# A decoder's merged attention stage: the output bias as a product of a row of ones on TensorE, in place of additions to the residual stream by GpSimd

## The chip, the cores and the metric

The kernel runs on one core of a Trainium2 chip. The metric is the device time of one execution in microseconds (us), the lower the better. The engines are TensorE (PE, with its weight loads shown apart as PEld), VectorE (DVE), ScalarE (ACT), GpSimd (POOL) and SyncE (SP), which issues most of the DMAs.

## The reference, cut to what matters

The program is a decoder of two layers on x of 8 batches x 512 tokens x 256 features. Each layer has an attention, a cross attention and a mixture of experts, each added to the residual stream x. The change lies in the second layer's cross attention, which has 16 heads of 16 features:

```python
    x = x + _L1_attn_ref(_layernorm(x, axis=-1), L1_attn_A, L1_attn_BC)
    x = x + _L1_xattn_ref(ctx_1024, ctx_1024, _layernorm(x, axis=-1), mask, Wv, Wk, Wq, Wo, bo)
...
    # in _L1_xattn_ref: v, k, q are heads of the three inputs, multiplied by Wv, Wk, Wq
        energy = jnp.einsum('nqhd,nkhd->nhqk', q, k)
        energy = jnp.where(mask == 0, jnp.float32(-1e+20), energy)
        attention = jax.nn.softmax(energy / jnp.sqrt(jnp.float32(E)), axis=3)
        out = jnp.einsum('nhql,nlhd->nqhd', attention, v).reshape(N, q_len, H * D)
        out = out @ Wo.T + bo
```

The vector `bo` of 256 numbers is the bias. Between the layers of the program the residual x stays in SBUF in float32, as 32 tiles of 128 tokens x 256 features, four to a batch.

## The kernel before, in words

Five stages follow one another: a first attention, a second one by correlation (stage two below, `mix_correlation`), routed experts, `mix_heads` (the stage of the change, about 945 to 1685 us of the profiled span) and the last experts.

`mix_heads` merges three things. It gathers the outputs of the routed experts into x (indirect DMAs issued by GpSimd), it runs the second layer's recurrence and adds it to x, and it runs the cross attention. Every engine has its own program, written out by hand, and they meet through semaphores that only count up.

The work goes batch by batch (8), in each batch by four groups g of four heads, in each group by eight steps n. At a step TensorE does two units of second energies (keys by queries, line 1105, into the PSUM tile `slim` of three slots, which ACT turns into exponentials, line 1278) and, between them, a pair of first energies for work half a group ahead (line 1094, into the PSUM tile `wide` of two slots, from which DVE takes row maxima, line 1349). After steps 1, 3, 5 and 7 it multiplies exponentials and values (line 1117; four products side by side, each on 32 of the array's columns). The table constants of lines 741 to 751 place everything else between these steps: `PREP_AT` prepares the next batch, `REC_AT` is the recurrence of the batch after the next, and `FIN_AT` = ((1, 1), (1, 4), (2, 1)) finishes the batch before. So in each batch b, `finish(b - 1)` on TensorE (lines 1135 to 1150) turns the heads' outputs in group 1, step 1; does output products for two tiles in group 1, step 4; and for the other two in group 2, step 1. I call the last two **output steps**: there are two a batch, 16 in all. In each of them TensorE does, for two tiles j, two products of 128x128 by 128x256 in float32 (line 1148) that add up in PSUM. A float32 product is two TensorE instructions in the trace, so an output step is 8 of them. DVE then adds the 128x512 result to x (line 1374) and takes statistics of it (line 1378). The last batch's three finishing items stand behind all other work (lines 1228 to 1231).

`wide` has two slots that are used in turn by energies, preparation, finishing and recurrence. TensorE waits before each use for the engine that empties the slot (`wide_freed`, line 807).

The bias is loaded by SP (line 920) as 128 copies of the 256 numbers. GpSimd adds it to the four tiles of a batch in x (`add_bias`, lines 995 to 1000). For batch 0 that stands between its part of the preparation and the gathers (line 1034); for batch b + 1 it stands at the end of group 3 of batch b (line 1053), behind `max_rows`. The latter is the end of a chain: DVE's maxima, split by GpSimd in three bfloat16 parts (lines 1008 to 1014), turned by TensorE (line 1125), copied by DVE (line 1355), and sent by a DMA on GpSimd's queue (line 1020) into the rows that the next group's second energies read. DVE waits for the addition in its `finish` (line 1372).

At the same place, in group 3, steps 5 to 7 of batches 0 to 5, DVE computes means and variances for the next normalization (`mean_of` and `var_of`, lines 1408 to 1422: short instructions in a chain, each waiting for the one before), ACT takes the root (line 1298) between two loads of its function table, and DVE goes on with a reciprocal and the normalizations (lines 1428, 1324).

Stage two already adds its own output bias as a product, for each of 8 batches: `nc.tensor.matmul(o, ones[0:1, :], bo[:], start=False, stop=True)` (line 553) behind two products of 128 rows (line 552), all in float32 with 256 columns.

Of the kernel before, what the change touches and what calls it, by code (L numbers as in the profile page):

```python
# [16 lines left out]
P = 128  # L17
B, S, D = 8, 512, 256
NT = B * S // P
TB = S // P  # L20
DC = D // P
# [638 lines left out]
def mix_heads(nc, ctx, x, ident, ident_bf, stats, mean, rstd, ctx_in, mask_in, w_vT, w_kT, w_qT, w_oT, b_o, part_rows, mask_dram,  # L660
# [6 lines left out]
    with ExitStack() as own:  # L667
        k = Kit(nc, own, "hd_")
        s = Kit(nc, ctx, "hd_")
        H, DH = 16, 16  # L670
        GH = 4
        NG = H // GH
# [12 lines left out]
        wq = k.sb("wq", [P, P])  # L685
        wv = k.sb("wv", [P, P])
        wo = k.sb("wo", [P, DC, D])
        bias = k.sb("bias", [P, D])
        parts = k.sb("parts", [P, 2, 3, DC, S], BF16)
        rest = k.sb("rest", [P, 2, DC, S])  # L690
        k_stack = k.sb("k_stack", [ROWS, 2, H, S], BF16)
# [1 line left out]
        zero = k.sb("zero", [P, 1])  # L693
# [9 lines left out]
        nparts = k.sb("nparts", [P, 2, P // (GH * TB), GH * TB], BF16)  # L703
        nrows = k.sb("nrows", [3 * GH * TB, 2, P], BF16)
        prob = k.sb("prob", [P, NUNIT, S])
        ones_bf = prob[0:ROWS - MASK_ROW, 0, :].bitcast(BF16)[:, 0:S]
# [6 lines left out]
        wide = k.ps("wide", [P, 2, 2, S])  # L713
        slim = k.ps("slim", [P, 3, S])
        pv = k.ps("pv", [P, S])
        zeroed, loaded, blocks_ready, weights_ready = s.sem("zeroed"), s.sem("loaded"), s.sem("blocks_ready"), s.sem("weights_ready")
        ones_ready, ones_loaded = s.sem("ones_ready"), s.sem("ones_loaded")
        ctx_loaded = s.sem("ctx_loaded")
        xn_ready, bias_added = s.sem("xn_ready"), s.sem("bias_added")
        wide_full, turned_ready, v_ready, maxed = s.sem("wide_full"), s.sem("turned_ready"), s.sem("v_ready"), s.sem("maxed")  # L720
        part0_ready, rest_ready, part1_ready, part2_ready = s.sem("part0_ready"), s.sem("rest_ready"), s.sem("part1_ready"), s.sem("part2_ready")
        stored, stacked, masked = s.sem("stored"), [s.sem(f"stacked{g}") for g in range(NG)], s.sem("masked")
# [8 lines left out]
        mask_loaded, rec_loaded, out_loaded = s.sem("mask_loaded"), s.sem("rec_loaded"), s.sem("out_loaded")  # L731
# [148 lines left out]
        with nc.Block() as block:  # L880
            @block.sync
            def _(sp):
# [34 lines left out]
                sp.dma_start(mask, mask_in.rearrange("b x y s -> (b x y) s")).then_inc(mask_loaded, 16)  # L917
                sp.dma_start(wbc[:], w_bc.rearrange("(c p) n -> p c n", p=P)).then_inc(rec_loaded, 16)
                sp.dma_start(decay[:], decay_in.rearrange("(c p) -> p c", p=P), allow_slow_non_contiguous=True).then_inc(rec_loaded, 16)
                sp.dma_start(bias[:], b_o.rearrange("(a n) -> a n", a=1).to_broadcast([P, D])).then_inc(out_loaded, 16)  # L920
                sp.dma_start(wo[:], w_oT.rearrange("(c p) n -> p c n", p=P)).then_inc(out_loaded, 16)

                sp.wait_ge(zeroed, 1)
# [39 lines left out]
            def _(pool):  # L963
# [28 lines left out]
                    pool.wait_ge(part1_ready, b * 2 + a + 1)  # L992
                    nc.gpsimd.tensor_tensor(parts[:, a, 2], rest[:, a], parts[:, a, 1], ALU.subtract).then_inc(part2_ready, 1)

                def add_bias(b):

                    pool.wait_ge(xn_ready, b * TB + TB)
                    for j in range(TB):
                        last = nc.gpsimd.tensor_tensor(x[:, b * TB + j, :], x[:, b * TB + j, :], bias[:], ALU.add)
                    last.then_inc(bias_added, 1)  # L1000

                def split_max(bt, g):

                    m, p = nmax[:, g % 2], nparts[:, g % 2].rearrange("p n (h c) -> p n h c", h=GH)
                    at = (bt.b * NG + g) * 3
                    z = zero[:].unsqueeze(2).to_broadcast([P, GH, TB])
                    pool.wait_ge(maxed, (bt.b * NG + g) * NSTEP + NSTEP)
                    nc.gpsimd.tensor_tensor(p[:, 0], m, z, ALU.add).then_inc(nstep, 1)
                    pool.wait_ge(nstep, at + 1)
                    nc.gpsimd.tensor_tensor(nrest[:], m, p[:, 0], ALU.subtract).then_inc(nstep, 1)  # L1010
                    pool.wait_ge(nstep, at + 2)
                    nc.gpsimd.tensor_tensor(p[:, 1], nrest[:], z, ALU.add).then_inc(nstep, 1)
                    pool.wait_ge(nstep, at + 3)
                    nc.gpsimd.tensor_tensor(p[:, 2], nrest[:], p[:, 1], ALU.subtract).then_inc(nparts_ready, 1)
# [8 lines left out]

                ALL = TB * TOP
                gathered_rows(0, range(TB))
                pool.wait_ge(zeroed, 3)
                pool.wait_ge(ones_loaded, 32)
                pool.wait_ge(mask_stored, 16)
                pool.sem_inc(passed, 1)
                gathered_rows(1, range(TB))  # L1030
                third_part(0, 0)
                pool.wait_ge(out_loaded, 32)
                third_part(0, 1)
                add_bias(0)
                gathers(2, 0, ALL // 2)
                split_max(Batch(0, 0), 0)
                max_rows(Batch(0, 0), 0)
                for b in range(B):
                    bt, nxt = Batch(b, b % 2), Batch(b + 1, (b + 1) % 2)
                    for g in range(NG):  # L1040
                        if g < NG - 1:
                            split_max(bt, g + 1)
                            max_rows(bt, g + 1)
                        elif b < B - 1:
                            split_max(nxt, 0)
                            max_rows(nxt, 0)
                        if g == 0 and b == 0:
                            gathers(2, ALL // 2, ALL)
                        if g == 0 and b < B - 1:
                            third_part(b + 1, 0)  # L1050
                            third_part(b + 1, 1)
                        if g == NG - 1 and b < B - 1:
                            add_bias(b + 1)
                        if bt.gathers and g < NG - 1:
                            gathers(b + 3, (0, 6, 13)[g], (6, 13, ALL)[g])
                for sem in nrows_loaded:
# [3 lines left out]
            def _(pe):  # L1060
# [74 lines left out]
                def finish(b, slot, n, at):  # L1135

                    if n == 0:
                        pe.wait_ge(turned, b * NG + NG)
                        for c in range(DC):
                            for qc in range(TB):  # L1140
                                last = nc.tensor.transpose(wide[:, at, c, qc * P:(qc + 1) * P], o[:, slot, qc, c * P:(c + 1) * P], ident[:])
                    else:
                        pe.wait_ge(out_loaded, 32)
                        pe.wait_ge(out_turned, b + 1)
                        for j in range(2):
                            qc = 2 * (n - 1) + j
                            for c in range(DC):
                                last = nc.tensor.matmul(wide[:, at, 0, j * D:(j + 1) * D], oT2[:, c, qc * P:(qc + 1) * P], wo[:, c, :],
                                                        start=(c == 0), stop=(c == DC - 1))
                    last.then_inc(wide_full, 1)  # L1150

                def combine(r, item, at):
# [167 lines left out]
            def _(dve):  # L1320
# [3 lines left out]
                        nc.vector.tensor_scalar(xn[:, j, :], x[:, t, :], mean[:, bass.ds(t, 1)], rstd[:, bass.ds(t, 1)],  # L1324
                                                ALU.subtract, ALU.mult).then_inc(xn_ready, 1)

                for t, value in ((ones_bf, 1.0), (nparts[:], 0.0), (zero[:], 0.0)):
                    nc.vector.memset(t, value).then_inc(zeroed, 1)
                dve.wait_ge(loaded, 3 * 16)
                dve.wait_ge(blocks_ready, 3)  # L1330
# [37 lines left out]

                def finish(b, n, uses, at):
                    dve.wait_ge(wide_full, uses + 1)  # L1370
                    if n == 1:
                        dve.wait_ge(bias_added, b + 1)
                    xs = x[:, bass.ds(b * TB + 2 * (n - 1), 2), :].rearrange("p j n -> p (j n)")
                    nc.vector.tensor_tensor(xs, xs, wide[:, at, 0, :], ALU.add).then_inc(x_done, 1)
                    dve.wait_ge(x_done, b * 2 + n)
                    for j in range(2):
                        t = b * TB + 2 * (n - 1) + j
                        nc.vector.bn_stats(stats[:, t, :], x[:, t, :]).then_inc(stats_done, 1)
# [1332 lines left out]
```

## Time and profile before

| | |
|---|---|
| median of 3 runs | 2698.16 us (2696.84 to 2705.11) |
| the profiled execution's own time | 2706.32 us |
| its span in the profile | 2704.3 us |
| PE busy | 2299.8 us (85%), 12186 instructions |
| PEld busy | 1627.9 us (60%) |
| DVE busy | 1270.6 us (47%) |
| ACT busy | 848.1 us (31%) |
| POOL busy | 866.2 us (32%) |

Times of the trace count from the start of the span. A slice of the page is 67.6 us. In the windows view, the numbers behind a stretch are its length and then the busy time and number of instructions of PE, PEld, DVE, ACT and POOL, the clock granted to TensorE as a share of 2.4 GHz, the share of the DMA engines and GB/s. In a timeline, a line gives start and length in us, engine, source line, operation, output and inputs, how many instructions were merged, and in brackets the idle time of the engine before it with what ended it. Matmul instructions overlap, so their pace is read from starts.

### The profile page before, as it was taken

The numbers are of one execution on the slowest core, as the hardware profiler recorded it, in microseconds if no ns is written. First come the engines' busy times: TensorE is split into PE (matmuls) and PEld (weight loads), VectorE is DVE, ScalarE is ACT, GpSimd is POOL, SyncE is SP. The second block draws the span as 40 slices with busy tenths as digits, with TensorE's granted clock in tenths as the row PEclk, the third lists the DMA queues.
The fourth block names the chain that finished last, engine by engine and source line by source line (L and its number), as shares of the span: only waits on it lengthen the run. The fifth ranks groups of instructions, "written<-read, shape, count | busy, mean of one in ns | idle before, by whom it ended". The sixth has DMA issues, their size and how long they took to land. (4 is left out here: it accounts for less than half of the span.)

```text
span 2704.3 us, 39994 instructions
## 1 busy us (share of the span) xinstructions
PE 2299.8 (85%) x12186; PEld 1627.9 (60%) x12187; DVE 1270.6 (47%) x2717; ACT 848.1 (31%) x1915; POOL 866.2 (32%) x1109
## 2 busy tenths in 40 slices
PE   6998856673999926698888887999999999999998
PEld 3454834442777722243333333655589999999998
DVE  5554135344444446677677765379322222222222
ACT  2222202220444403455565565322212222222221
POOL 2000003563000043654344121122235444445544
PEclk9999656886999967899899999999999999999999
DMA  9993116222555543544334220410047777777775
GB/s 338 372 365 133 58 28 249 86 95 81 157 156 156 152 125 83 106 111 101 71 73 102 67 72 13 162 39 16 16 139 245 246 245 245 246 249 247 247 246 168
DMA packets 246074, 412.60 MB, mean 153 GB/s; under 512 B 29958, under 2 KB 223855, under 8 KB 237784
## 3 DMA queue, kind: packets, MB, share of 16 engines
q1 hardware_dynamic: 206040, 351.70, 38.4%
q0 software_dynamic: 39936, 59.70, 10.7%
q8 instruction: 49, 0.80, 0.1%
q14 instruction: 49, 0.40, 0.0%
HBM read 261.83 MB, written 148.89 MB: 152 GB/s over the span
## 5 line engine op out<-in xcount | busy, mean ns | idle before, releaser
L2544 PE MATMUL me_hp<-me_xgT,me_w 128*128 128x160 f32 x3072 | 440.2, 300 | 0.6 <-DVE me_xgT L2586 0.6
L2544 PEld LDWEIGHTS me_hp<-me_xgT,me_w 128*128 128x128 f32 x3072 | 424.6, 191 | 1.5 <-DVE me_xgT L2586 0.7
L1349 DVE TENSOR_REDUCE hd_nmax<-hd_wide 128x2 f32<-128x1024 f32 x256 | 307.7, 1219 | 128.5 <-PE hd_wide L1094 124.3
L1278 ACT ACTIVATE hd_prob<-hd_slim 128x512 f32<-128x512 f32 x512 | 276.2, 601 | 190.4 <-PE hd_slim L1105 157.6
L2600 DVE TENSOR_TENSOR me_hid<-me_act_out,me_hp 128x160 f32<-128x160 f32 x384 | 123.5, 322 | 371.8 <-ACT me_act_out L2572 354.2
L1105 PE MATMUL hd_slim<-hd_q_stack,hd_k_stack 100*128 100x512 bf16 x512 | 199.9, 394 | 43.1 <-ACT hd_prob L1278 32.8
L2553 PE MATMUL me_op<-me_hid,me_w 128*128 128x160 f32 x1536 | 235.9, 303 | 0.0
L1094 PE MATMUL hd_wide<-hd_k_stack,hd_q_stack 97*128 97x512 bf16 x512 | 201.3, 398 | 29.5 <-DVE hd_rest L1343 15.9
L2572 ACT ACTIVATE me_act_out<-me_hp 128x160 f32<-128x160 f32 x384 | 116.8, 304 | 346.0 <-PE me_hp L2544 346.0
L2553 PEld LDWEIGHTS me_op<-me_hid,me_w 128*128 128x128 f32 x1536 | 213.7, 190 | 2.6
L1105 PEld LDWEIGHTS hd_slim<-hd_q_stack,hd_k_stack 100*128 100x128 bf16 x512 | 50.2, 99 | 197.7 <-ACT hd_prob L1278 84.7
L1977 PE MATMUL mr_e_hp<-mr_w,mr_e_xtT 128*128 x640 | 167.9, 385 | 0.8 <-issue 0.8
L2244 PE MATMUL me_r_hp<-me_r_xnT,me_r_sw 128*128 128x512 f32 x384 | 167.5, 592 | 0.0
L977 POOL DMA_INDIRECT all_x<-outputs,rt_place x96 | 150.2, 1565 | 28.4 <-issue 28.4
L1665 POOL DMA_INDIRECT places<-mr_s_xg,mr_s_place x128 | 124.9, 976 | 89.5 <-DVE mr_s_place L1825 50.4
L1117 PE MATMUL hd_pv<-hd_prob,hd_v 128*32 128x512 f32 x1024 | 137.7, 610 | 3.9 <-ACT hd_oT L1241 3.6
L2202 POOL TENSOR_TENSOR me_r_hid<-me_r_act_out,me_r_up_out 128x512 f32<-128x512 f32 x48 | 64.5, 1345 | 211.6 <-ACT me_r_up_out L2300 211.6
L2490 POOL DMA_INDIRECT out_x<-me_oa,me_then_a x64 | 104.1, 1626 | 69.5 <-POOL me_then_b L2096 35.7
L2244 PEld LDWEIGHTS me_r_hp<-me_r_xnT,me_r_sw 128*128 128x128 f32 x384 | 72.3, 190 | 84.6 <-issue 84.2
L2033 DVE TENSOR_TENSOR mr_e_hid<-mr_e_act_out,mr_e_hp 128x128 f32<-128x128 f32 x160 | 46.1, 288 | 153.7 <-ACT mr_e_act_out L2009 153.7
L1977 PEld LDWEIGHTS mr_e_hp<-mr_w,mr_e_xtT 128*128 128x128 f32 x640 | 110.4, 193 | 10.5 <-issue 1.5
L2574 ACT ACTIVATE me_oT<-me_op 128x320 f32<-128x320 f32 x64 | 28.0, 437 | 242.1 <-PE me_op L2553 242.1
(384 smaller groups left out, 3731.2 us busy)
## 6 DMA issues: line engine op xcount, KB each, us to landing
me_w<-in_L_ffn_w_exp SPq DMA_DIRECT2D x64, 2304.0 KB
places<-z_zero SPq DMA_DIRECT2D x64, 1152.0 KB, 11.2
mr_e_xt<-places SPq DMA_DIRECT2D x160, 144.0 KB, 2.2
outputs<-mr_e_y SPq DMA_DIRECT2D x160, 128.0 KB, 1.7
part_rows<-hd_parts SPq DMA_DIRECT2D x48, 256.0 KB
hd_k_stack<-part_rows SPq DMA_DIRECT2D x192, 64.0 KB
hd_q_stack<-part_rows SPq DMA_DIRECT2D x192, 64.0 KB
mr_w<-in_L_ffn_w_in SPq DMA_DIRECT2D x4, 2048.0 KB
```

Of the source, the lines that this page charges most:

```text
L977: nc.gpsimd.indirect_dma_start(out=x[:, r * TB + j, :], out_offset=None, in_=outputs[:, :], in_offset=bass.IndirectOffsetOnAxis(ap=place[: ...
L1094: last = nc.tensor.matmul(wide[:, at, j, :], q_stack[0:FIRST_ROWS, bt.slot, h, qc * P:(qc + 1) * P], k_stack[0:FIRST_ROWS, bt.slot, h, :], ...
L1105: nc.tensor.matmul(slim[:, slim_slot(bt, item), :], k_stack[:, bt.slot, h, kc * P:(kc + 1) * P], q_stack[:, bt.slot, h, :], start=True, st ...
L1117: last = nc.tensor.matmul(pv[32 * j:32 * j + 32, :], v[:, slot, kc, head(g, j), :], prob[:, kc * GH + j, :], start=(kc == 0), stop=(kc == ...
L1278: nc.scalar.activation(prob[:, u, :], slim[:, slim_slot(bt, item), :], ACT.Exp, scale=D ** -0.5)\
L1349: nc.vector.tensor_reduce(nmax[:, g % 2, n // 2, c:c + 2], wide[:, at], AX.X, ALU.max, negate=True)\
L1665: nc.gpsimd.indirect_dma_start(out=places[:, :], out_offset=bass.IndirectOffsetOnAxis(ap=place[:, b * TB + j, n:n + 1], axis=0), in_=xg[:, ...
L1977: last = nc.tensor.matmul(hp[:, v, 0:2 * F], xtT[:, v, c, :], w1[:, bass.ds(e, 1), c, :].rearrange("p a n -> p (a n)"), start=(c == 0), st ...
L2244: last = nc.tensor.matmul(hp[:, u % 2, half, :], sw1[:, c, at:at + P], xnT[:, c, b * S:(b + 1) * S], start=(c == 0), stop=(c == DC - 1))
L2544: last = nc.tensor.matmul(hp[:, f % 3, half * CAP:(half + 1) * CAP], w1[:, sl, c, cols], xgT[:, sl, c, :], start=(c == 0), stop=(c == DC - 1))
L2553: last = nc.tensor.matmul(op[:, c, 0:CAP], w2[:, sl, f, c * P:(c + 1) * P], hid[:, sl, f, :], start=(f == 0), stop=(f == FC - 1))
L2600: nc.vector.tensor_tensor(hid[:, sl, f, :], act_out[:, f % 2, :], hp[:, f % 3, 0:CAP], ALU.mult).then_inc(h_free, 1)
```

## The change

The bias and a new row of 128 ones have one partition each. DVE sets the ones (a fourth small memset), SP loads the bias once. GpSimd's additions, their semaphore and DVE's wait for it go. In each output step TensorE begins each of its two sums with a product of the row of ones (1x128) and the bias (1x256), in float32, as in stage two.

```diff
-        bias = k.sb("bias", [P, D])
+        bias = k.sb("bias", [1, D])
+        one_row = k.sb("one_row", [1, P])
...
-        xn_ready, bias_added = s.sem("xn_ready"), s.sem("bias_added")
+        xn_ready = s.sem("xn_ready")
...
-                sp.dma_start(bias[:], b_o.rearrange("(a n) -> a n", a=1).to_broadcast([P, D])).then_inc(out_loaded, 16)
+                sp.dma_start(bias[:], b_o.rearrange("(a n) -> a n", a=1)).then_inc(out_loaded, 16)
...
-                def add_bias(b):
-
-                    pool.wait_ge(xn_ready, b * TB + TB)
-                    for j in range(TB):
-                        last = nc.gpsimd.tensor_tensor(x[:, b * TB + j, :], x[:, b * TB + j, :], bias[:], ALU.add)
-                    last.then_inc(bias_added, 1)
-
...
-                pool.wait_ge(zeroed, 3)
+                pool.wait_ge(zeroed, 4)
...
                 third_part(0, 0)
-                pool.wait_ge(out_loaded, 32)
                 third_part(0, 1)
-                add_bias(0)
                 gathers(2, 0, ALL // 2)
...
-                        if g == NG - 1 and b < B - 1:
-                            add_bias(b + 1)
...
+                        pe.wait_ge(zeroed, 4)
                         pe.wait_ge(out_loaded, 32)
                         pe.wait_ge(out_turned, b + 1)
                         for j in range(2):
+                            nc.tensor.matmul(wide[:, at, 0, j * D:(j + 1) * D], one_row[:], bias[:], start=True, stop=False)
                             qc = 2 * (n - 1) + j
                             for c in range(DC):
                                 last = nc.tensor.matmul(wide[:, at, 0, j * D:(j + 1) * D], oT2[:, c, qc * P:(qc + 1) * P], wo[:, c, :],
-                                                        start=(c == 0), stop=(c == DC - 1))
+                                                        start=False, stop=(c == DC - 1))
...
-                for t, value in ((ones_bf, 1.0), (nparts[:], 0.0), (zero[:], 0.0)):
+                for t, value in ((ones_bf, 1.0), (nparts[:], 0.0), (zero[:], 0.0), (one_row[:], 1.0)):
...
                     dve.wait_ge(wide_full, uses + 1)
-                    if n == 1:
-                        dve.wait_ge(bias_added, b + 1)
```

## Rows read from the trace of the kernel before

**Rows 1.** The page in 40 slices: PE busy and granted clock, in tenths.

```profile
PE   6998856673999926698888887999999999999998
...
PEclk9999656886999967899899999999999999999999
```

**Rows 2.** Windows: us, busy us (x) per engine, granted clock, DMA share, GB/s.

```profile
1180.00:1260.00 80.00, 68.67 (x364) 30.38 (x361) 57.45 (x82) 46.53 (x81) 38.30 (x47) 0.96 0.41 92
```

**Rows 3.** Line and tile views: duration ns (min/median/max), first and last start.

```profile
L1148 PE MATMUL hd_wide<-hd_wo,hd_oT x128: 377/379/483, 1182.1 to 1683.4; 128*128 128x256 f32 x128
...
L999 POOL TENSOR_TENSOR all_x<-all_x,hd_bias x32: 716/738/769, 1025.8 to 1619.7; 128x256 f32<-128x256 f32 x32
```

**Rows 4.** Timeline at a first output step: start, us, engine, line, operation, [idle before].

```profile
1262.65 1.89 PE L1148 MATMUL hd_wide<-hd_wo,hd_oT 128*128 128x256 f32 x8
...
1264.38 0.60 PE L1132 MATMUL hd_slim<-all_ident,hd_oT 128*128 128x128 f32 x4
...
1266.38 0.65 PE L1157 MATMUL hd_wide<-all_ident,hd_xn 128*128 128x128 f32 x4 [0.53 <-DVE all_x L1374]
```

**Rows 5.** Timeline at the second output step of the same batch.

```profile
1276.05 1.99 PE L1148 MATMUL hd_wide<-hd_wo,hd_oT 128*128 128x256 f32 x8 [0.44 <-DVE hd_nmax L1349]
...
1277.97 1.06 PE L1117 MATMUL hd_pv<-hd_prob,hd_v 128*32 128x512 f32 x8
```

**Rows 6.** Timeline and window of stage two, where a bias is already a product.

```profile
393.59 1.22 PE L553 MATMUL xa_proj<-xa_bo,xa_ones 1*128 1x256 f32 x2
...
396.74 1.22 PE L553 MATMUL xa_proj<-xa_bo,xa_ones 1*128 1x256 f32 x2
...
398.00:402.00 4.00, 4.00 (x8) 2.40 (x9) 3.67 (x11) 0.00 (x0) 0.00 (x0) 0.50 0.00 0
```

**Rows 7.** Timeline of DVE at the start of the attention stage.

```profile
959.09 0.29 DVE L1332 TENSOR_TENSOR hd_wk<-hd_wk,hd_blocks 128x128 f32<-128x128 f32 x1 [5.26 <-DMA hd_wv<-in_L_xattn_WvT]
```

**Rows 8.** DVE groups, 1100 to 1660 us: busy, mean ns; then L1414 alone.

```profile
L1413 DVE TENSOR_SCALAR all_mean<-all_mean (+2 forms) x6 | 3.6, 605 | 0.2
...
L1414 DVE TENSOR_TENSOR hd_half_diff<-all_stats 128x8 f32 (+2 forms) x6 | 3.9, 650 | 0.2
...
L1415 DVE SCALAR_TENSOR_TENSOR hd_half_diff<-hd_half_diff 128x8 f32<-128x8 f32 (+1 forms) x6 | 3.8, 636 | 0.2
...
L1421 DVE SCALAR_TENSOR_TENSOR hd_var<-hd_var,hd_half_diff 128x8 f32<-128x8 f32 (+1 forms) x6 | 1.4, 239 | 0.2
...
L1414 DVE TENSOR_TENSOR hd_half_diff<-all_stats x11: 165/643/656, 981.1 to 1545.2; 128x4 f32<-128x4 f32 x6, 128x8 f32 x4, 128x8 f32<-128x8 f32 x1
```

**Rows 9.** Timeline where a bias addition meets the end of a batch.

```profile
1222.74 2.77 POOL L999 TENSOR_TENSOR all_x<-all_x,hd_bias 128x256 f32<-128x256 f32 x4
...
1226.74 0.21 ACT L1298 ACTIVATE hd_dev<-hd_var 128x8 f32<-128x8 f32 x1 [2.90 <-DVE hd_var L1422]
...
1228.91 0.61 PE L1105 MATMUL hd_slim<-hd_q_stack,hd_k_stack 100*128 100x512 bf16 x1 [2.25 <-ACT hd_prob L1278]
```

**Rows 10.** Timeline at the first bias addition; below it the same DVE form undisturbed.

```profile
1024.34 3.84 DVE L1436 TENSOR_SCALAR hd_xn<-all_x,all_mean,all_rstd 128x256 f32<-128x256 f32 x4
...
1028.33 1.09 PE L1157 MATMUL hd_wide<-all_ident,hd_xn 128*128 128x128 f32 x4 [8.37 <-DVE hd_xn L1436]
...
1228.00 1.38 DVE L1324 TENSOR_SCALAR hd_xn<-all_x,all_mean,all_rstd 128x256 f32 x4
```

**Rows 11.** Window and GpSimd timeline behind two ends of a batch.

```profile
1304.00:1322.00 18.00, 12.14 (x44) 5.73 (x41) 9.13 (x15) 8.64 (x14) 1.94 (x3) 0.62 0.11 34
...
1302.43 0.70 POOL L1020 DMA_DIRECT2D hd_q_stack<-hd_nrows  x1
...
1332.54 0.65 POOL L1020 DMA_DIRECT2D hd_q_stack<-hd_nrows  x1
...
1466.59 0.71 POOL L1020 DMA_DIRECT2D hd_q_stack<-hd_nrows  x1
...
1492.13 0.66 POOL L1020 DMA_DIRECT2D hd_q_stack<-hd_nrows  x1
```

## The prediction

> **What bounds the kernel now.** I began with the page's slices. The stage of the change is slices 16 to 25: TensorE is busy for 80 to 90% of nearly every one, at close to full clock [rows 1]. A window of one steady batch says the same: PE 68.7 of 80 us, against 57.5 for DVE, 46.5 for ACT and 38.3 for POOL [rows 2]. So work added to TensorE is suspected of costing its full length, and work taken from GpSimd of being worth nothing by itself. Whether that holds is a matter of the two places where the work lies, so I read those in the timeline next.
>
> At an output step TensorE has no gap: the 8 instructions start at 1262.65 and the next work, turning a group's output, follows at 1264.38. 2.00 us later, at 1266.38, TensorE has waited 0.53 us for DVE's addition to x [rows 4]. That addition reads what TensorE wrote and stands on DVE behind the normalization of the group just turned. A later end of the output step makes turning, DVE and this wait later by the same amount; it doesn't fill the gap. At the second output step TensorE waits 0.44 us before it, for a slot that DVE empties, and the new products wait for that slot too [rows 5]. I find no event behind an output step that TensorE waits for and that doesn't itself follow from TensorE's work.
>
> At the ends of batches, GpSimd's addition is not the bystander that its idle time suggests. It starts at 1222.74, while DVE is in its chain of statistics [rows 9], and three of these instructions, of 8 columns each, take 605 to 650 ns on the mean where the undisturbed ones take 165 [rows 8]. ACT waits 2.90 us for the end of that chain, then loads its table, and TensorE waits 2.25 us for ACT's first exponential [rows 9]. So here GpSimd's work is on the path.
>
> **What the change adds.** Two products in each of 16 output steps (128 instructions of line 1148 are 16 steps of 8 [rows 3]) are 32 products, 64 instructions of 256 columns in float32. Undisturbed such an instruction takes (1264.38 - 1262.65) / 8 = 0.216 us [rows 4]: 0.86 us a step, 13.8 us in all.
>
> They have one row where their neighbours have 128 (or 97). Stage two shows what such a product costs between products of 128 rows: a batch of 4 + 2 instructions takes 396.74 - 393.59 = 3.15 us, at a granted clock of 0.50, that is 1.2 GHz [rows 6]. At that clock six instructions should take 6 x 0.432 = 2.59 us. The 0.56 us left are two changes of shape, 0.28 us each. The nearest row at full clock (2.4 GHz) is the output step that begins behind a wait, with its weights not loaded ahead, and ends at line 1117, whose products use 32 columns each: 1277.97 - 1276.05 = 1.92 us for 8 instructions, 0.19 more than 8 x 0.216 [rows 5]. A change of shape seems to have both of these, loads that aren't ahead and a gap, and the clock of the output steps is full, so I take 0.19. Bounds: nothing (no row excludes it at 2.4 GHz) and 0.28 (if it is a fixed time). An output step has four changes (into the row, out, in, out), 0.76 us, 12.2 us over 16 steps. The sum added is 13.8 + 12.2 = **26.0 us**, from 13.8 to 31.7.
>
> By the Trainium skill, "TensorEngine Tiling (Array Packing)", section "Key Properties", changing the tiling mode makes TensorE drain. Its page "TensorE: Matmul & The Clock Gate", section "Single matmul latency", puts a drain at some 175 ns; by that estimate the 64 changes would add 11.2 us. The rows of stage two agree that there is such a price; no row here shows it with one row at full clock.
>
> All of it lies on the path by the reading above, the last batch's two steps too, behind which only DVE works. The wait for the ones is passed long before; nothing is queued behind it that could run. The memset is the fourth of DVE's small ones, and DVE idles 5.26 us behind them for weights; without that cover it would cost under 0.1 us [rows 7]. GpSimd waits for it at a point far ahead of its next use. The smaller load of the bias costs nothing and gives nothing: no one but the first output step, 200 us later, needs it now. DVE's wait that goes was met each time, since the addition lies more than a batch before it.
>
> **What it removes.** GpSimd loses 32 x 0.738 = 23.6 us of work [rows 3], which is worth what it held up:
> - The statistics of batches 0 to 5. The excess over 0.165 us is 2.6 + 2.9 + 2.8 + 0.4 = 8.8 us (6 x 0.440, 0.485, 0.471, 0.074) [rows 8]. In batch 5, whose chain starts before the addition, one instruction of line 1414 is slowed by the issue of a DMA by GpSimd and stays so, 0.5 us by the mean of its line: 8.3 us. It is on the path through ACT to TensorE [rows 9]. With the chain 1.4 us shorter (0.44 + 0.485 + 0.47) the next thing late is still ACT's table and the exponential, 0.85 us of the 2.25 us wait being left, so I take it all. Bounds: 0 and 8.3 us.
> - The first addition. DVE's four normalizations take 3.84 us, undisturbed 1.38, and TensorE waits for them [rows 10]. They begin under another instruction of GpSimd, which stays; from its end at about 1025.9 the last three need 1.0 us instead of 2.3. I take 1.1 us, between 0 and 2.5.
>
> The gathers that GpSimd issues behind the first addition start 3 us earlier; those that DVE waits for in batch 0 stand behind a later DMA of maxima, and gain nothing of it. The sum removed is **9.4 us**.
>
> **The clock** may move either way. Behind the ends of batches it falls; in the worst window (18 us) it averages 0.62, with PE busy for 12.14 us [rows 11]. From one DMA of maxima to the next this boundary takes 1332.54 - 1302.43 = 30.1 us, another 25.5 [rows 11]. A stall shorter by 1.4 us might avoid the fall; a shift of the work against it might lengthen it. With 30.1 against 25.5 as the ends, six boundaries hold some 12 us to be regained at best (4.6 from the worst, an estimated 1.5 from each other), and about as much to be lost. I take 0.
>
> **Sum:** 26.0 - 9.4 = +16.6 us; against the profiled execution's 2706.3 us that is 2722.9. This execution was 8.2 us over the median of the runs shown, and I put the difference to the median: 2698.2 + 16.6 = **2714.8 us**, 0.6% slower. A measurement of this kernel can tell about 0.3%, 8.1 us, from no change.
>
> **Rivals.**
> - *The products are absorbed.* TensorE idles 11 us in a batch [rows 2]; if its stalls at the end of a batch (2.25 us for ACT and others [rows 9]) are set by DVE, ACT and DMAs rather than by its own progress, the 3.2 us a batch vanish in them. Then only the removed 9.4 us show: 2688.8 us, **faster**. It decides the sign from 64% absorbed (26.0 x 0.36 = 9.4) and passes -0.3% where all but 1.3 us is. Against it: the statistics and maxima that set those stalls wait for TensorE's energies of the same group, which shift too. 6%.
> - *A change of shape costs nothing at full clock.* Then 13.8 - 9.4 = +4.4 us: 2702.6, no change that can be told. For it: the only rows with one row are at half clock. Against it: the gap at line 1117, which is at full clock [rows 5]. 13%. By the Trainium skill, "TensorE: Matmul & The Clock Gate", section "Why this matters for your kernels", a single product of 32 rows takes as long as one of 128; that would be this case.
> - *The clock comes back.* The shorter stalls keep TensorE at 2.4 GHz: 16.6 - 12 = +5 us, 2703. It needs the falls behind most ends of a batch to go. 9%.
> - *The dear change.* 0.28 us each at any clock: 31.7 - 9.4 = +22.3 us, 2720.5. 12%.
>
> **How the numbers follow.** The forecast has 60%. Its own range, with the clock at +-6 us and the gains at their lower bounds in part, is 2707 to 2722. To leave out no more than 2 in 10 the range takes in the cheap change and the regained clock below, and the dear change with some loss of clock above: 2702 to 2725. Slower by over 0.3% (above 2706.3): the forecast but for a twelfth of it, the dear change, and part of the regained clock, 69%. Within 0.3%: 26%. Faster by over 0.3%: the absorbed case but for its last part, 5%.
>
> **What the next profile should show.** Line 1148's 128 instructions unchanged, and 64 new ones of 1x256; an output step from its first start to the next work of about 3.4 us instead of 1.73 (2.6 if the change of shape is free); POOL's busy time down by 24 us; the statistics' instructions at 165 to 185 ns; TensorE's wait for the exponential at the end of a batch about 1.5 us shorter; the batch as a whole about 1.8 us longer. The forecast is wrong if the output step grows by 1.6 us and the batch doesn't (absorbed), if it grows by 0.9 (cheap change), or if the windows behind the ends of batches have another clock.

## The result and the profile after

| | before | after |
|---|---|---|
| median, 13 runs each on one chip | 2699.9 us (2692.8 to 2707.5) | 2719.1 us (2707.0 to 2732.2) |
| ratio to before, 95% interval | | 1.0068 (1.0048 to 1.0088) |
| profiled execution, its span | 2706.3, 2704.3 us | 2722.1, 2719.8 us |

The change costs 18.4 us (13.0 to 23.8) by the ratio and 15.5 us by the two spans. The page of the changed kernel, busy times and slices:

```profile
PE 2323.3 (85%) x12250; PEld 1633.4 (60%) x12251; DVE 1260.3 (46%) x2718; ACT 847.3 (31%) x1915; POOL 842.3 (31%) x1077
...
PE   6998856674999835788888888899999999999998
...
PEclk9999566886999957999999999899999999999999
```

GpSimd is busy for 23.9 us less, TensorE for 23.5 us more. The slices of the stage look like [rows 1]: little of it is visible at this scale but the clock, whose two slices of 0.8 in the stage before now read 0.9, and which has a slice of 0.8 behind the stage's end. So I went to the same four places as before.

**The output steps**, in TensorE's timeline of the changed kernel (first and second output step of one batch), and the tile view of the new products:

```profile
1259.10 0.38 PE L1084 MATMUL hd_wide<-hd_k_stack,hd_q_stack 97*128 97x512 bf16 x1
1259.40 0.69 PE L1137 MATMUL hd_wide<-hd_bias,hd_one_row 1*128 1x256 f32 x2
1260.03 1.13 PE L1140 MATMUL hd_wide<-hd_wo,hd_oT 128*128 128x256 f32 x4
1261.09 0.69 PE L1137 MATMUL hd_wide<-hd_bias,hd_one_row 1*128 1x256 f32 x2
1261.71 1.13 PE L1140 MATMUL hd_wide<-hd_wo,hd_oT 128*128 128x256 f32 x4
1262.68 0.60 PE L1122 MATMUL hd_slim<-all_ident,hd_oT 128*128 128x128 f32 x4
...
1274.35 0.69 PE L1137 MATMUL hd_wide<-hd_bias,hd_one_row 1*128 1x256 f32 x2 [0.44 <-DVE hd_nmax L1341]
...
1277.72 1.07 PE L1107 MATMUL hd_pv<-hd_prob,hd_v 128*32 128x512 f32 x8
```

```profile
L1137 PE MATMUL hd_wide<-hd_bias,hd_one_row x64: 374/478/792, 1178.0 to 1697.1; 1*128 1x256 f32 x64
```

From the first start to the next work, the first step takes 1262.68 - 1259.40 = 3.28 us, in place of 1.73 [rows 4]; the second takes 3.37, in place of 1.92 [rows 5]. The wait of 0.44 us ahead of the second is still there, unchanged. The starts within the first step show where the time beyond the columns goes: from the two instructions of one row to the next work it is 0.63 us, 0.20 more than 2 x 0.216, and from the four of 128 rows to the next pair 1.06 us, 0.20 more than 4 x 0.216. Either shape pays when it follows the other, so this is a price of the change and not of a product of one row by itself.

**The statistics of DVE**, groups of 1100 to 1660 us of the changed kernel (busy, mean ns):

```profile
L1403 DVE TENSOR_SCALAR all_mean<-all_mean (+2 forms) x6 | 1.0, 174 | 0.2
L1404 DVE TENSOR_TENSOR hd_half_diff<-all_stats 128x8 f32 (+2 forms) x6 | 1.0, 172 | 0.2
...
L1405 DVE SCALAR_TENSOR_TENSOR hd_half_diff<-hd_half_diff 128x8 f32<-128x8 f32 (+1 forms) x6 | 1.0, 167 | 0.2
```

They took 605, 650 and 636 ns before [rows 8]. **The end of a batch**, in the timeline of the changed kernel, with the DMA of maxima at three ends of a batch; the line of before's GpSimd timeline that answers to the first of them stands below it:

```profile
1222.46 0.70 POOL L1014 DMA_DIRECT2D hd_q_stack<-hd_nrows  x1
...
1225.73 0.21 ACT L1290 ACTIVATE hd_dev<-hd_var 128x8 f32<-128x8 f32 x1 [1.45 <-DVE hd_var L1412]
...
1227.90 0.39 PE L1095 MATMUL hd_slim<-hd_q_stack,hd_k_stack 100*128 100x512 bf16 x1 [1.73 <-ACT hd_prob L1270]
...
1302.19 0.70 POOL L1014 DMA_DIRECT2D hd_q_stack<-hd_nrows  x1
...
1331.06 0.65 POOL L1014 DMA_DIRECT2D hd_q_stack<-hd_nrows  x1
...
1469.39 0.71 POOL L1014 DMA_DIRECT2D hd_q_stack<-hd_nrows  x1
...
1493.71 0.66 POOL L1014 DMA_DIRECT2D hd_q_stack<-hd_nrows  x1
```

```profile
1222.01 0.71 POOL L1020 DMA_DIRECT2D hd_q_stack<-hd_nrows  x1
```

ACT waits 1.45 us for the statistics, not 2.90 [rows 9]. From the DMA to the energies behind ACT's first exponential it is 1227.90 - 1222.46 = 5.44 us; before it was 1228.91 - 1222.01 = 6.90 [rows 9]. That is 1.46 us less for one end of a batch.

**The start and the tail of the stage**: DVE's first normalizations and TensorE behind them, then the last batch's output steps, in the changed kernel's timeline; below, before's last output steps.

```profile
1022.69 2.72 DVE L1426 TENSOR_SCALAR hd_xn<-all_x,all_mean,all_rstd 128x256 f32<-128x256 f32 x4
...
1025.56 1.94 PE L1149 MATMUL hd_wide<-all_ident,hd_xn 128*128 128x128 f32 x8 [7.11 <-DVE hd_xn L1426]
...
1688.78 0.67 PE L1137 MATMUL hd_wide<-hd_bias,hd_one_row 1*128 1x256 f32 x2 [1.21 <-ACT hd_oT L1259]
...
1697.69 2.08 PE L1140 MATMUL hd_wide<-hd_wo,hd_oT 128*128 128x256 f32 x4
```

```profile
1680.09 3.69 PE L1148 MATMUL hd_wide<-hd_wo,hd_oT 128*128 128x256 f32 x16 [1.20 <-ACT hd_oT L1267]
```

The last two output steps took 3.69 us and now take 1699.77 - 1688.78 = 11.0 us. The windows of the changed kernel (columns as in [rows 2]) show a second reason beside the products: the clock is 0.61 there, the third line.

```profile
1180.00:1260.00 80.00, 69.54 (x368) 28.99 (x366) 55.75 (x82) 46.67 (x81) 34.60 (x42) 0.98 0.40 89
1304.00:1322.00 18.00, 12.61 (x52) 6.01 (x52) 7.97 (x14) 9.42 (x16) 0.00 (x0) 0.72 0.10 34
1688.00:1700.00 12.00, 10.98 (x24) 5.79 (x24) 1.64 (x4) 0.64 (x1) 0.00 (x0) 0.61 0.00 0
```

So the trace of the change already holds both halves of the forecast: a longer output step and a shorter end of a batch. What it can't show is how much of the 18.4 us each is worth, since one execution differs from another by several us in stages that the change doesn't touch. That is what the runs below are for.

### The profile page after: what moved, and what is told of

Same layout as the page of the kernel before. It is cut to its first block and busy times, and to the rows that moved or that the text cites. A ratio compares the mean times of both kernels' runs of the same rounds, so it can differ in the third digit from the quotient of the medians.

```text
span 2719.8 us, 40098 instructions
## 1 busy us (share of the span) xinstructions
PE 2323.3 (85%) x12250; PEld 1633.4 (60%) x12251; DVE 1260.3 (46%) x2718; ACT 847.3 (31%) x1915; POOL 842.3 (31%) x1077
## 6 DMA issues: line engine op xcount, KB each, us to landing
mr_e_xt<-places SPq DMA_DIRECT2D x160, 144.0 KB, 2.1
```

## The experiments

My theory: the products cost their full length, a good part of which is the change of shape to one row and back, and the end of GpSimd's collision with DVE gives back some 10 us. The rivals: the gain is larger than the collision (the clock comes back) and the products dearer; or a bias product costs its columns alone, and the rest of the time is something else. Experiments 1 to 4 ran on one chip, where before took 2700.4 us (29 runs); 5 and 6 on another, where the same kernel took 2652.9 us (11 runs). Only ratios are carried from one to the other.

### 1. The additions taken away, no products

```diff
-                            nc.tensor.matmul(wide[:, at, 0, j * D:(j + 1) * D], one_row[:], bias[:], start=True, stop=False)
...
-                                                        start=False, stop=(c == DC - 1))
+                                                        start=(c == 0), stop=(c == DC - 1))
```

Against the changed kernel. Nothing adds the bias: this part of the computation is left out.

> The changed kernel without its products of the row of ones, so that no one adds the bias: GpSimd's additions are gone and TensorE's program is that of before. The output lacks the bias in every token. It measures the gain of the removal alone. By my sum: the statistics 8.3 us and the first addition 1.1 us, so 9.4 us faster than before, about 2690. By the traces compared (the ends of batches were 14.7 us shorter in all, the stretch before the first batch about 1.4 us), with falls of the clock that went away: 14 to 17 us faster, about 2684. By the rival for which GpSimd's idle time shows that its work is hidden: no change, 2700. The statistics' instructions take 165 to 175 ns in either of the first two.

Measured: 2688.4 us (12 runs), ratio 0.9963 (0.9945 to 0.998), that is -10.0 us (-14.9 to -5.4). The statistics are at 172 ns, in DVE's groups of this kernel:

```profile
L1403 DVE TENSOR_TENSOR hd_half_diff<-all_stats 128x8 f32 (+2 forms) x6 | 1.0, 172 | 0.2
```

So the additions, which ran on an engine that is idle for two thirds of the time, cost about 10 us. The forecast's 9.4 us holds. Of the rival's 14 to 17 us the interval leaves only the lowest part: 17 is out, 14 just isn't.

### 2. The additions kept, and products of a row of zeros besides

```diff
+        no_row = k.sb("no_row", [1, P])
...
+                            nc.tensor.matmul(wide[:, at, 0, j * D:(j + 1) * D], no_row[:], bias[0:1, :], start=True, stop=False)
...
-                                                        start=(c == 0), stop=(c == DC - 1))
+                                                        start=False, stop=(c == DC - 1))
```

Against the kernel before. The zeros are a fourth memset; the sums don't change.

> The kernel before, with all its additions, plus a product of a row of zeros and the bias ahead of each of the 32 sums: the cost of the products alone. By my sum 26.0 us slower, 2726. If TensorE's stalls absorb them: under 10 us slower. If the products also lower the clock, as the changed kernel's last output steps suggest (11.0 us instead of 3.7 where the sum has 7.0): 28 to 35 us slower. An output step of group 1 takes 3.28 us at full clock, one of group 2 3.37 us.

Measured: 2728.4 us (6 runs), ratio 1.0107 (1.0085 to 1.0129), +28.9 us (23.0 to 34.8). TensorE's timeline at a second output step, and DVE's group of the statistics, in this kernel:

```profile
1279.57 0.69 PE L1148 MATMUL hd_wide<-hd_bias,hd_no_row 1*128 1x256 f32 x2 [0.44 <-DVE hd_nmax L1352]
...
1282.94 1.06 PE L1118 MATMUL hd_pv<-hd_prob,hd_v 128*32 128x512 f32 x8
```

```profile
L1417 DVE TENSOR_TENSOR hd_half_diff<-all_stats 128x8 f32 (+2 forms) x6 | 3.9, 650 | 0.2
```

The step is the changed kernel's (3.37 us), the statistics are before's (650 ns). The two halves add up: 28.9 - 10.0 = 18.9 us, and the whole change measures 18.4. Each half is known to some 5 us, so a third effect larger than that isn't there; a smaller one isn't excluded. Between 26.0 and the rival's 28 to 35 us the interval doesn't decide.

### 3. Products of 128 rows in place of one

```diff
-        bias = k.sb("bias", [1, D])
-        one_row = k.sb("one_row", [1, P])
+        bias = k.sb("bias", [P, D])
+        one_row = k.sb("one_row", [P, P])
...
-                sp.dma_start(bias[:], b_o.rearrange("(a n) -> a n", a=1)).then_inc(out_loaded, 16)
+                sp.dma_start(bias[:], b_o.rearrange("(a n) -> a n", a=1).to_broadcast([P, D])).then_inc(out_loaded, 16)
...
-                for t, value in ((ones_bf, 1.0), (nparts[:], 0.0), (zero[:], 0.0), (one_row[:], 1.0)):
+                for t, value in ((ones_bf, 1.0), (nparts[:], 0.0), (zero[:], 0.0), (one_row[:], 1.0 / P)):
```

Against the changed kernel: 128 rows of 1/128 by 128 copies of the bias. The instructions are as many and have as many columns; only the shape is that of their neighbours.

> The changed kernel with 128 rows of 1/128 and the bias on all 128 partitions, float32 as before: the same number of instructions and columns, but no change of shape. If the change of shape is what an instruction of one row costs beyond its columns, an output step takes 1.73 + 0.86 = 2.6 us in group 1 and 2.8 us in group 2, 11 us less over 16 steps: about 7 us slower than before, 2707. If the clock also stops falling behind output steps and in the last ones, 14 to 18 us less than the changed kernel: equal to before within 4 us. If the price comes from something else (accumulating on a third product, the semaphore wait), no change against the changed kernel: 18 us slower than before.

Measured: 2705.5 us (12 runs), ratio 1.0025 (1.0009 to 1.004), +6.8 us (2.4 to 10.8); 11.6 us less than the whole change. TensorE's timeline of this kernel at a first output step:

```profile
1253.71 0.38 PE L1084 MATMUL hd_wide<-hd_k_stack,hd_q_stack 97*128 97x512 bf16 x1
1253.93 0.60 PE L1137 MATMUL hd_wide<-hd_bias,hd_one_row 128*128 128x256 f32 x2
...
1256.52 0.60 PE L1122 MATMUL hd_slim<-all_ident,hd_oT 128*128 128x128 f32 x4
```

The step takes 1256.52 - 1253.93 = 2.59 us: 12 instructions of 0.216. Against the changed kernel's 3.28, and 0.22 instead of 0.30 us from the last energies to it, the row shape costs 0.69 + 0.08 = 0.77 us in a first output step, 0.19 for each of four changes. Nothing else differs in what TensorE does, so more rows, and with them 128 times the arithmetic, are cheaper than one.

### 4. One row still, but two changes of shape in a step instead of four

```diff
-        bias = k.sb("bias", [1, D])
+        bias = k.sb("bias", [1, 2, D])
...
-                sp.dma_start(bias[:], b_o.rearrange("(a n) -> a n", a=1)).then_inc(out_loaded, 16)
+                sp.dma_start(bias[:], b_o.rearrange("(a j n) -> a j n", a=1, j=1).to_broadcast([1, 2, D])).then_inc(out_loaded, 16)
...
+                        nc.tensor.matmul(wide[:, at, 0, :], one_row[:], bias[:].rearrange("a j n -> a (j n)"), start=True, stop=False,
+                                         skip_group_check=True)
                         for j in range(2):
-                            nc.tensor.matmul(wide[:, at, 0, j * D:(j + 1) * D], one_row[:], bias[:], start=True, stop=False)
```

Against the changed kernel: one product of 512 columns for both tiles. The columns are the same.

> The changed kernel with the bias stored twice in its row and one product of 512 columns a step in place of two of 256: as many columns, half the changes of shape. By the price per change (0.17 to 0.19 us each, two fewer a step) an output step is 0.35 us shorter, 5.5 us in all: 13 us slower than before, 2713. If the price is per product and not per change, the same 5 us; if it lies in the columns (a product of one row streams slowly), nothing. The pace inside the product tells the last two apart: 0.43 us between the starts of its two instructions at full clock, if it streams as others do.

Measured: 2709.9 us (12 runs), ratio 1.0033 (1.0012 to 1.0055), +8.9 us (3.2 to 14.8). TensorE's timeline of this kernel:

```profile
1253.36 0.38 PE L1084 MATMUL hd_wide<-hd_k_stack,hd_q_stack 97*128 97x512 bf16 x1
1253.67 1.12 PE L1136 MATMUL hd_wide<-hd_bias,hd_one_row 1*128 1x512 f32 x2
1254.72 1.99 PE L1141 MATMUL hd_wide<-hd_wo,hd_oT 128*128 128x256 f32 x8
1256.55 0.60 PE L1122 MATMUL hd_slim<-all_ident,hd_oT 128*128 128x128 f32 x4
```

2.88 us: 0.40 less than the changed kernel, for two changes fewer, 0.20 each. Over 16 steps that is 6.3 us of the 9.5 by which the medians' ratios differ; the intervals take in the rest. The two instructions of one row take 1254.72 - 1253.67 = 1.05 us for 1024 columns, which is 4 x 0.216 and one change: their columns are no slower than others. Experiment 4 by itself can't tell a price for each change from one for each product, since it halves both. The starts in the changed kernel's output step do, and experiment 3 shows that as many products without a change of shape cost their columns alone.

### 5. The additions kept on GpSimd, but moved out of DVE's way

```diff
-                def add_bias(b):
+                def add_bias(b, normed):
...
-                    pool.wait_ge(xn_ready, b * TB + TB)
+                    pool.wait_ge(xn_ready, normed)
...
-                add_bias(0)
...
                 max_rows(Batch(0, 0), 0)
+                add_bias(0, 2 * TB)
...
-                            add_bias(b + 1)
+                            add_bias(b + 1, min(b + 3, B) * TB)
```

Against the kernel before. If the 10 us of experiment 1 are the collision and not GpSimd's work as such, they are to be had with all 32 additions in place: they only have to start behind DVE's normalization of the next batch.

> The kernel before with GpSimd's additions kept, each moved behind the next batch's normalization, where DVE is in none of its statistics; TensorE has no product for the bias. If the gain of the removal (10.0 us measured) was the collision with DVE's chain of statistics, it comes back in full here although GpSimd does all its work: 8 to 11 us faster than before, 2690, and the statistics' instructions take 165 to 180 ns. If it came from GpSimd having less to do at all (its queue, its DMAs), no change against before. If the additions now stand in the way of the third parts or the splits of maxima that follow on GpSimd, slower than before by up to 2.8 us a batch.

Measured: 2640.6 us (5 runs) against 2652.9, ratio 0.9962 (0.9948 to 0.9976), -10.1 us (-13.8 to -6.4). DVE's group of the statistics; GpSimd's timeline at an end of a batch, in this kernel:

```profile
L1414 DVE TENSOR_TENSOR hd_half_diff<-all_stats 128x8 f32 (+2 forms) x6 | 1.0, 172 | 0.2
```

```profile
1160.56 0.70 POOL L1020 DMA_DIRECT2D hd_q_stack<-hd_nrows  x1
1166.58 2.77 POOL L999 TENSOR_TENSOR all_x<-all_x,hd_bias 128x256 f32<-128x256 f32 x4 [5.31 <-DVE hd_xn L1324]
...
1184.68 0.65 POOL L1020 DMA_DIRECT2D hd_q_stack<-hd_nrows  x1
```

The same 2.77 us of additions, 5.3 us later, and the whole gain of experiment 1. From one DMA to the next it takes 24.1 us. By the ratios this version is faster than both kernels of the case.

### 6. The product in its cheapest shape

```diff
-        bias = k.sb("bias", [1, D])
-        one_row = k.sb("one_row", [1, P])
+        bias = k.sb("bias", [P, D])
+        bias_rows = k.sb("bias_rows", [P, 2, D], BF16)
+        one_row = k.sb("one_row", [P, P], BF16)
...
+                        nc.tensor.matmul(wide[:, at, 0, :], one_row[:], bias_rows[:].rearrange("p j n -> p (j n)"), start=True, stop=False,
+                                         skip_group_check=True)
                         for j in range(2):
-                            nc.tensor.matmul(wide[:, at, 0, j * D:(j + 1) * D], one_row[:], bias[:], start=True, stop=False)
...
+                    steps.link(nc.vector.tensor_copy(part[:, 0], bias[:]))
+                    steps.link(nc.vector.tensor_tensor(rest[:, 0], bias[:], part[:, 0], ALU.subtract))
+                    steps.link(nc.vector.tensor_copy(part[:, 1], rest[:, 0]))
+                    steps.link(nc.vector.tensor_tensor(rest[:, 1], rest[:, 0], part[:, 1], ALU.subtract))
+                    steps.link(nc.vector.tensor_scalar(rest[:, 0], part[:, 0], ident[:, 0:1], None, ALU.mult))
+                    steps.link(nc.vector.scalar_tensor_tensor(rest[:, 0], part[:, 1], ident[:, 1:2], rest[:, 0], ALU.mult, ALU.add))
+                    steps.link(nc.vector.scalar_tensor_tensor(rest[:, 0], rest[:, 1], ident[:, 2:3], rest[:, 0], ALU.mult, ALU.add))
+                    steps.link(nc.vector.tensor_copy(bias_rows[:, 0], rest[:, 0]))
+                    steps.tick(nc.vector.tensor_copy(bias_rows[:, 1], rest[:, 0]))
```

Against the changed kernel. Once, at the stage's start, DVE splits the bias into three bfloat16 parts and puts them in rows 0, 1 and 2 of a tile of 128 rows, the others zero. With ones in bfloat16 a step then has one instruction of 512 columns, without a change of shape.

> The changed kernel with the bias product in its cheapest form: the bias split once in three bfloat16 parts that stand in rows 0 to 2 of a tile of 128 rows (the rest zero), two copies side by side, against a full tile of ones in bfloat16: one instruction of 512 columns a step, no change of shape. An output step takes 0.22 us more than before, 3.5 us over 16 steps, and the removal gives 10: 6 to 7 us faster than before, 2693, and 25 us faster than the changed kernel. The nine short instructions of DVE that make the parts lie in its wait for weights and gathers at the start of the stage and cost at most 3 us. If the mere presence of a third product in the sum costs time, not its columns and its shape, an output step grows by over 0.5 us and the gain is under 2 us.

Measured: 2639.7 us (6 runs) against 2652.9, ratio 0.9959 (0.9944 to 0.9974), -10.9 us (-14.9 to -6.9). TensorE's timeline of this kernel, and the tile view of the new operand's loads (15 of the 16 instructions themselves are missing from the records):

```profile
1204.78 0.38 PE L1086 MATMUL hd_wide<-hd_k_stack,hd_q_stack 97*128 97x512 bf16 x1
1205.21 1.89 PE L1144 MATMUL hd_wide<-hd_wo,hd_oT 128*128 128x256 f32 x8
1206.94 0.60 PE L1124 MATMUL hd_slim<-all_ident,hd_oT 128*128 128x128 f32 x4
```

```profile
L1139 PEld LDWEIGHTS hd_wide<-hd_bias_rows,hd_one_row x16: 95/95/98, 1126.5 to 1615.7; 128*128 128x128 bf16 x16
```

From the last energies to the first product of line 1144 it is 0.43 us, where experiment 3's first two lines stand 0.22 apart: the instruction adds 0.21 us to a first output step. Around a second one it adds 0.13: from one DMA of maxima to the next it is 20.10 us there and 19.97 in experiment 5, which has no product. That is 2.7 us in all, not the 3.5 expected, and would leave 10.0 - 2.7 = 7.3 us of gain. The interval, 6.9 to 14.9, holds that at its lower end; most of it lies above the 6 to 7 us expected, and why isn't explained. The gain isn't distinguishable from experiment 5's, and by the ratios this version too is faster than both kernels of the case.

## Why the prediction was right, step by step

The forecast was slower, by 16.6 us, to 2714.8; measured were 2719.1 us and +18.4 (13.0 to 23.8).

- **TensorE has no room at the output steps**: right. Neither step absorbed any of the products, and the wait of 0.44 us ahead of the second kept its length. The absorbed case is out by experiment 2.
- **Products, 13.8 us**: right. Experiment 3 shows 0.216 us for each of its 12 instructions in a step.
- **Changes of shape, 0.19 us each, 12.2 us**: right in the price, one too many in every second step. In the first step the four cost 0.19 each (experiment 3). The second step grew by 3.37 - 1.92 = 1.45 us, 0.86 of it columns, and the 0.59 left are three changes. The fourth was paid before already: it is the very 0.19 from which the forecast took its price [rows 5]. Counted in the trace of the change, seven batches of 1.55 + 0.08 + 1.45 = 3.08 us and an estimated 3.2 us at full clock for the last steps make 24.8 us, beside the forecast's 26.0 and experiment 2's 28.9 (23.0 to 34.8). The cheap case, 13.8, and the dear one as a fixed 0.28 us at any clock are out, both by the steps of 3.28 and 2.88 us. The ones' memset takes 0.165 us where under 0.1 was forecast; it still lies in DVE's wait for the weights.

The Trainium skill says in "TensorEngine Tiling (Array Packing)", section "Key Properties", that changing the tiling mode drains TensorE. The trace agrees with a price at such a change, close to the 175 ns that the Trainium skill has for a drain in "TensorE: Matmul & The Clock Gate", section "Single matmul latency"; that the 0.19 us are this drain is not shown. By the Trainium skill, the same page, section "Why this matters for your kernels", a single product of 32 rows takes as long as one of 128. Here, with one row, that holds for the columns (experiment 4) but not for a product between others of 128 rows.

- **The statistics, 8.3 us, and the first addition, 1.1 us**: right, with one misreading. Experiment 1 shows 10.0 us for both, the end of a batch shows 1.46 us less where 1.4 were forecast, and the first four normalizations take 2.72 instead of 3.84 us [rows 10], 1.12 less. Experiment 5 shows that the gain is the collision's: it comes in full with all additions in place. The misreading: I took 0.5 us of batch 5 for the work of a DMA issue and kept it. In the changed kernel the same instruction lies wholly under the same issue and takes 0.17 us. Its two timelines there, DVE's and GpSimd's:

```profile
1549.89 0.17 DVE L1404 TENSOR_TENSOR hd_half_diff<-all_stats 128x4 f32<-128x4 f32 x1
```

```profile
1549.78 0.62 POOL L1014 DMA_DIRECT2D hd_q_stack<-hd_nrows  x1
```

So that 0.5 us went as well, and the sum of the collision should have been 8.8.

- **The clock, 0 by choice between -12 and +12**: the term without a reading of its own, and that 0 served was luck. In the two profiled executions the clock moved both ways. The six ends of a batch (DMA of maxima to the next) take 158.9 us before and 144.0 after, 14.9 less, of which the chain explains 8.8. In the profiles of the experiments they take 158.6 us with the collision (2), and without it 146.3 (1), 146.4 (3), 147.8 (4), 146.2 (5) and 143.3 (6). So wherever the collision is gone some 2 to 7 us beyond the chain come back (5 and 6 ran on the other chip). In the change the worst went from 30.1 [rows 11] to 28.9 us, with its window's clock from 0.62 to 0.72.

  Against that, the clock fell in output steps. In the changed kernel two of the seven stretches around a second output step take 23.0 us from DMA to DMA where the others like them take 21.4 (from 1185.60 to 1208.60, for one, with a clock of 0.74 from 1196 to 1202), which is 3.2 us. The last output steps grew by 7.3 us, an estimated 3.2 for the products and 4.1 for the clock of 0.61. With the counted terms, 24.8 + 3.2 + 4.1 - 14.9 - 1.1 = 16.1 us, the 15.5 us between the two spans are nearly all named. Experiment 1, which has no bias product, fell in the last steps too; its window and timeline:

```profile
1650.00:1655.00 5.00, 4.33 (x12) 3.53 (x13) 1.02 (x2) 0.52 (x1) 0.00 (x0) 0.66 0.00 0
```

```profile
1650.67 5.38 PE L1139 MATMUL hd_wide<-hd_wo,hd_oT 128*128 128x256 f32 x16 [1.21 <-ACT hd_oT L1258]
```

  So a fall in the last steps isn't the products' doing alone. But the three kernels with products of one row (the change, 2 and 4) have the lowest mean clocks over these steps, 0.59, 0.60 and 0.63, where experiment 1 has 0.68, 3 has 0.76 and before, 5 and 6 have 1.00. They are also the only ones with a fall around a second output step of the seven batches before: two, one and one, and none in the five other profiles. One profile of each isn't proof, so that such products bring falls with them is not shown; it would explain why experiment 2 measured 28.9 us where the steps count 24.8. How large the clock's shifts are in most of the 13 runs, and what makes a fall come in one execution and not in another, stays open.

- **A batch 1.8 us longer**: the two batches from 1302 to 1469 us take 1469.39 - 1302.19 = 167.2 us, before 164.2 [rows 11], 1.5 us each. In that sum are falls of the clock that went and one that came, so it isn't the chain and the steps alone. That the 80 us window shows TensorE busy for only 0.9 us more than [rows 2] is no sign against it: the window holds another piece of the batch.
- **TensorE's wait for the exponential 1.5 us shorter**: by its name it fell from 2.25 to 1.73 us only. The other 0.9 us went from waits ahead of it, as the 1.46 us from DMA to energies show. I had named the wrong wait for the right amount.

No step of the sum failed by more than 1.3 us but the clock's, whose shifts of several us each cancelled; the forecast is right in its mechanism and owes part of its closeness to that. The 1.8 us between forecast and measurement are less than the interval's half width.

## What to carry to other kernels

An engine that is mostly idle can still be on the path, through what its instructions do to a neighbour's: look at what runs beside its work before calling it free, and move the work by a few us before moving it to the engine that bounds the kernel. A bias as a product costs its columns and the changes of the array's shape around it; give it the rows of its neighbours, one instruction in bfloat16 parts if the precision allows, and it costs 0.2 us instead of 1.6. Take both halves apart, cost removed and cost added, each in a kernel of its own: here -10.0 and +28.9 us add up to the +18.4 of the whole, within their intervals.

## What the runs showed of the hardware that was not expected

- A product of 1 row between others of 128 costs more than one of 128 at the same columns: 3.28 against 2.59 us for a step with two such products.
- GpSimd's additions hold up DVE's instructions of 4 and 8 columns on SBUF (0.17 to 0.65 us), but not DVE's maxima, which read PSUM. Whether it is PSUM or the kind of instruction that spares the maxima, no run here shows. Before's DVE timeline, in a stretch where GpSimd adds from 1545.77 to 1548.55:

```profile
1545.93 0.65 DVE L1415 SCALAR_TENSOR_TENSOR hd_half_diff<-hd_half_diff 128x4 f32<-128x4 f32 x1
1546.61 1.23 DVE L1349 TENSOR_REDUCE hd_nmax<-hd_wide 128x2 f32<-128x1024 f32 x1
...
1547.98 0.60 DVE L1421 SCALAR_TENSOR_TENSOR hd_var<-hd_var,hd_half_diff 128x4 f32<-128x4 f32 x1
```

The maxima take 1.23 us there and 1.22 elsewhere. By the Trainium skill, "SBUF — State Buffer", section "Who interferes with whom", the port pair that DVE shares with GpSimd is locked for a whole instruction; the trace agrees, since the small instructions take nearly the length of one addition (0.69 us).

- Two chips took 2700.4 and 2652.9 us for the same kernel, 1.8% apart, more than any effect of this study. Why isn't known.
